# A one added to the normalised input carries the biases, the first table comes back into the score rows, and the transposed second table is added there

## The chip, the cores and the metric

One core of a Trainium2 chip runs the whole program. The metric is the device time of one execution in microseconds (us). A core has five engines with queues of their own: TensorE (PE in the rows; PEld is its loading of weights), VectorE (DVE), ScalarE (ACT), GpSimd (POOL) and SyncE (SP), which issues most transfers between DRAM and the on-chip memory SBUF. TensorE writes into eight banks of another memory, PSUM (PS0 to PS7), which VectorE and ScalarE empty. Engines wait for one another by semaphores.

## The reference, cut to what matters

An image batch of 2 x 32 x 32 tokens with 64 channels goes through an attention-like block over windows of 8 x 8 tokens, and then through a mixture of eight experts. The first block, per window b, with 8 heads h of width 32 and P = 64 positions o, i:

```python
t = x @ W_prep + b_prep            # x normalised over its channels; t holds q_n, q, k, k_m, v
bias, pat_n, pat_m = _spatial(intrinsic)   # tables by the relative position of o and i
score = bias[None]
score = score + jnp.einsum('bhod,ohid->bohi', q_n, pat_n)     # second table
score = score + jnp.einsum('bhod,bhid->bohi', q, k)
score = score + jnp.einsum('bhid,ohid->bohi', k_m, pat_m)     # first table
mean, std = ...                    # over i, for each o and head
score = (score - mean) / std
out = jnp.einsum('bohi,bhid->bohd', score, v)
... out @ W_fin + b_fin, added to x; then the experts
```

The experts: layer norm, a router that keeps the best two of eight, two products with a GELU between them, a weighted sum, added to the input.

## The kernel before, in words

All 32 windows stay on the chip; two windows make a pair, so there are 16 pairs, in four groups of four. The program has these stages.

1. Head. The input XR comes in four parts on SP's queue; WS (weights), REL (tables) and WV on ScalarE's. VectorE computes mean and variance and a reciprocal root by Newton steps; VectorE (three parts) and ScalarE (one) write the normalised input XN. TensorE transposes the weights (L615), multiplies them into the first table (TAM, `table("tm")`, L520), transposes XN into XF (L628), and computes the rows that the biases add (`bias_terms`, L549 to L558). GpSimd spreads these rows (EB), writes them to DRAM, and SP and GpSimd load them back as BI in 16 small transfers (L316).
2. First table's products (L571 with TAM): 16 tiles of four positions, two at a time, each 128 x 512. ScalarE and VectorE copy them from PSUM to TMG, SP writes each tile to DRAM (`moved`, L339). When all are there (`moved_out`), SP reads them back in another order, rows by position, as TMS (L347): this is a transpose through DRAM. Between the tiles TensorE makes the second table (TAN, L520 and L527) and weight products (L540).
3. Second table's products (L571 with TAN), in eight rounds: two tiles, copied to TNT by ScalarE, mixed with key products (`mixed_keys`, L585, into Y), and the turning of the two tiles before (`turned`, L595: four transposes a tile). VectorE adds BI to each turned tile and writes the score rows SCN (L1099). Between them stand the centred input XC (L604) and a shift of the experts' bias (L507).
4. Score loop, one step per pair t, ordered by `pe_steps(t)`: values of a pair (L669, bank 6), scores of two pairs at every second step (L684, banks 0 and 1), weighted sums (L698). GpSimd adds TMS into SCN, pair after pair, 16 adds (L437). VectorE adds the scores and SCN to SR (L1158). ScalarE copies the values to BV (L974), squares SR (SQ, L980), copies the weighted sums to OR (L986). After every four pairs: sums of the squares (`ss`, L708), a copy by ScalarE (SSB, L993), their transposes (`st`, L760), the variances VB by VectorE, a power by GpSimd (RSC, L455), the scaled result ON by VectorE (L1178), its transposes, the last product, the second layer norm and the router. GpSimd's queue holds the power behind the 16 adds.
5. Experts, 16 rounds: hidden products (L719, L720), GELU by ScalarE (L938), second products (L731), gates. Its first round starts in the last step of the loop.

The order of each queue is that of the code. A use of a PSUM bank waits until the use before it is emptied; `make_plan` lists the uses in order and counts these waits.

## Time and profile before

| what | value |
|---|---|
| runs | 201.16, 201.94, 205.39 us; median 201.94 |
| profiled execution | 203.32 us, its span 201.5 us |
| mean granted TensorE clock | 0.975 |
| TensorE busy | 174.9 us (87%) |
| ScalarE busy | 117.9 us (59%) |
| VectorE busy | 108.1 us (54%) |
| GpSimd busy | 85.9 us (43%) |

The span goes from the first to the last instruction of the core; the time of the run holds what lies around it too. The busy share is a mean over stages with different limits: in one stage TensorE works without a gap, in another it waits for a power on GpSimd. The granted clock is that of TensorE: 1.00 is 2.4 GHz, 0.50 is 1.2.

### The profile page before, as it was taken

To read this page: it belongs to the slowest core of one execution; us is meant where nothing else is said; L and a number is where in the kernel's file an instruction comes from. 1 tells how busy PE (TensorE), PEld (TensorE's weight loads), DVE (VectorE), ACT (ScalarE), POOL (GpSimd) and SP (SyncE) were. 2 spreads that over 40 slices of the span, in tenths; PEclk is the share of its full clock that TensorE was granted. 3 is DMA by queue.
4 is the path that set the end of the run, shared out by engine and by line. 5 is a ranking of instruction groups with operands and counts; after the bars stand their busy time and mean duration, and the time that the engine had idled before them with its cause. 6 is when DMAs were issued, how large, how long until landed. Compare 5 with 4: busy or idle time off the path is not lost.

```text
span 201.5 us, 4321 instructions
## 1 busy us (share of the span) xinstructions
PE 174.9 (87%) x1582; PEld 108.6 (54%) x1582; DVE 108.1 (54%) x296; ACT 117.9 (59%) x233; POOL 85.9 (43%) x130
## 2 busy tenths in 40 slices
PE   0519999999998799936995999999999999999983
PEld 0417554654555575626854856575556665655531
DVE  1594258445546525207386955196928773874323
ACT  2244397446453798808596497546666566676730
POOL 6120549040001999993866638481910073031000
PEclk9999999999999999985999789999999999999999
DMA  6930276969991002000300000000000000000000
GB/s 146 245 119 0 90 239 210 335 163 220 220 218 23 0 3 88 20 0 3 102 5 0 2 5 0 0 0 0 3 26 0 0 3 28 0 2 0 29 0 26
DMA packets 10868, 12.96 MB, mean 64 GB/s; under 512 B 2512, under 2 KB 8216, under 8 KB 10848
## 3 DMA queue, kind: packets, MB, share of 16 engines
q1 hardware_dynamic: 9936, 11.73, 22.2%
q10 hardware_dynamic: 528, 0.85, 1.5%
q0 software_dynamic: 384, 0.11, 0.5%
q8 instruction: 13, 0.21, 0.4%
q14 instruction: 7, 0.06, 0.1%
HBM read 7.94 MB, written 4.75 MB: 63 GB/s over the span
## 4 chain that ended last, share of the span: by engine, by line
PE 67%; POOL 14%; DVE 8%; DMA 3%; issue 3%; ACT 3%; SPq 1%; DVEq 0%; ACTq 0%; POOLq 0%
PE PS L731 13%; POOL SCN L437 10%; PE PS L571 9%; PE PS L719 7%; PE PS L720 6%; PE PS L805 4%; PE PS L585 4%; PE PS L780 4%; PE PS L595 3%; DMA XR<-in_x 3%; POOL RSC L455 3%; PE PS L628 2%; PE PS L604 2%; PE PS L769 2%; PE PS L698 1%
## 5 line engine op out<-in xcount | busy, mean ns | idle before, releaser
L938 ACT ACTIVATE HR<-PS,B1P 128x512 f32<-128x512 f32 x64 | 39.0, 693 | 5.0 <-PE PS L720 4.9
L731 PE MATMUL PS<-HR,W2s 128*64 128x512 f32 x128 | 31.0, 605 | 0.0
L437 POOL TENSOR_TENSOR SCN<-SCN,TMS 128x512 f32<-128x512 f32 x16 | 19.7, 1284 | 21.7 <-DVE SCN L1099 21.7
L719 PE MATMUL PS<-X,W1H 128*128 128x512 f32 x64 | 27.5, 430 | 0.0
L720 PE MATMUL PS<-X,W1L 128*128 128x512 f32 x64 | 25.8, 404 | 0.0
L443 POOL COPY PW<-PG 128x512 f32<-128x512 f32 x16 | 10.4, 684 | 34.1 <-DVE PG L1187 33.9
L1019 ACT ACTIVATE GB<-PS 128x512 f32<-128x512 f32 x16 | 9.6, 598 | 23.0 <-PE PS L805 23.0
L455 POOL TENSOR_TENSOR RSC<-VB,NHALF 128x32 f32<-128x32 f32 x4 | 21.9, 5463 | 0.3
L1158 DVE TENSOR_TENSOR SR<-PS,SCN 128x512 f32<-128x512 f32 x16 | 10.7, 685 | 13.6 <-PE PS L684 11.5
L974 ACT ACTIVATE BV<-PS 64x256 f32<-64x256 f32 x32 | 12.2, 380 | 7.6 <-PE PS L669 7.3
L731 PEld LDWEIGHTS PS<-HR,W2s 128*64 128x64 f32 x128 | 7.8, 136 | 13.3 <-issue 12.3
L719 PEld LDWEIGHTS PS<-X,W1H 128*128 128x128 f32 x64 | 12.6, 197 | 3.2 <-issue 0.8
L1139 DVE SCALAR_TENSOR_TENSOR GM<-PS,B,GB 128x512 f32<-128x512 f32 x12 | 9.0, 751 | 9.3 <-ACT GB L1019 7.9
L720 PEld LDWEIGHTS PS<-X,W1L 128*128 128x128 f32 x64 | 12.7, 198 | 2.2
L921 ACT ACTIVATE TNT<-PS 128x512 f32<-128x512 f32 x16 | 8.7, 594 | 8.8 <-PE PS L571 8.8
L805 PEld LDWEIGHTS PS<-IDN,PW 128*128 128x128 f32 x64 | 6.7, 140 | 13.2 <-issue 13.2
L1078 DVE TENSOR_SCALAR Y<-PS,YB 128x512 f32<-128x512 f32 x8 | 6.2, 772 | 12.7 <-PE PS L585 12.7
L669 PE MATMUL PS<-WV,XC 64*64 64x128 f32 x128 | 10.6, 285 | 2.3 <-ACT BV L974 2.2
L980 ACT ACTIVATE SQ<-SR 128x512 f32<-128x512 f32 x16 | 10.1, 630 | 2.4 <-DVE SR L1158 2.1
L698 PE MATMUL PS<-BV,SR 128*64 128x66 f32 x256 | 11.2, 230 | 0.0
L805 PE MATMUL PS<-IDN,PW 128*128 128x128 f32 x64 | 10.5, 286 | 0.8 <-ACT GB L1019 0.8
L986 ACT ACTIVATE OR<-PS 128x264 f32<-128x264 f32 x16 | 6.2, 390 | 7.9 <-DVE ON L1178 5.9
(149 smaller groups left out, 321.8 us busy)
## 6 DMA issues: line engine op xcount, KB each, us to landing
moved<-TMG SPq DMA_DIRECT2D x16, 256.0 KB, 2.9
TMS<-moved SPq DMA_DIRECT2D x16, 256.0 KB, 8.0
W1R<-in_W SPq DMA_DIRECT2D x4, 256.0 KB, 4.0
XR<-in_x SPq DMA_DIRECT2D x4, 128.0 KB, 4.7
W1E<-in_W SPq DMA_DIRECT2D x2, 256.0 KB, 6.2
W2s<-in_W SPq DMA_DIRECT2D x1, 512.0 KB, 3.7
out<-XR SPq DMA_DIRECT2D x4, 128.0 KB, 1.8
REL<-in_rel ACTq DMA_DIRECT2D x2, 225.0 KB, 5.1
```

The lines of the kernel that those rows point to most:

```text
L437: G.tensor_tensor(pair, pair, TMS[:, t, :], ALU.add).then_inc(scn_ready, 1)
L455: G.tensor_tensor(RSC[:, :, :, :].rearrange("p q h g -> p (q h g)"), vb, NHALF[:, :], ALU.pow).then_inc(rsc_ready, 1)
L571: last = nc.tensor.matmul(PS[before[(kind, 2 * m + r)][0]][32 * u:32 * u + 32, :], XF[rows, :, token], window, start=True, stop=True)
L669: m = nc.tensor.matmul(ps[C * g:C * g + C, b * P:b * P + P], XC[rows, lo:lo + WT], WV[rows, g * P:g * P + P], start=True, stop=True)
L698: m = nc.tensor.matmul(dst, SR[t % 3][:, (2 * h + b) * C:(2 * h + b) * C + C], BV[t % 3][:, b, h, :, :].rearrange("p g d -> p (g d)"), sta ...
L719: nc.tensor.matmul(ps[:, :], W1H[:, col:col + P], X2[:, j * 512:j * 512 + 512], start=True, stop=False)
L720: end(nc.tensor.matmul(ps[:, :], W1L[:, col:col + P], X2[:, j * 512:j * 512 + 512], start=False, stop=True), "h", n)
L731: m = nc.tensor.matmul(ps[d * C:d * C + C, :], W2s[:, 2 * (2 * ep + d) + c, :], HR[(4 * u + 2 * c + d) % 8][:, :], start=(c == 0), stop=(c ...
L805: m = nc.tensor.transpose(ps[:, q * P:q * P + P], PW[:, a % 4, q, :, :].rearrange("p d c -> p (d c)"), IDN[:, :])
L938: A(HR[n % 8][:, :], PS[b][:, :], ACT.Gelu, bias=B1P[:, col:col + 1]).then_inc(bank_drained[b], 1)
L974: last = A(BV[tv % 3][g * C:g * C + C, :, :, g, 0:HD].rearrange("p b h d -> p (b h) d"), PS[6][g * C:g * C + C, 0:256].rearrange("p (n d) ...
L1158: V_.tensor_tensor(SR[t % 3][:, :].rearrange("p (h b o) -> p h b o", h=4, b=2), PS[t % 2][:, :].rearrange("p (h b o) -> p h b o", h=4, b=2 ...
```

## The change

The weights are centred (each channel of the input has mean zero over its 64 channels, so subtracting the mean over the channels from the weights changes no product) and get the bias divided by 64 in every row. XF is the normalised transposed input plus one, so that its products with the weights hold the bias. `bias_terms`, YB, EB, the DRAM scratch of the bias and its 17 transfers go. The position bias (RB) is added into the second table by TensorE with SEL. The second table is made before the input is transposed, in banks 4 to 7. The input's last two parts come on ScalarE's queue, the weights and tables on SP's; GpSimd normalises the last part.

The first table's tiles are read back from DRAM into SCN itself, not into TMS. The copies of the second table's products (TNT) take the memory of TMG, so TensorE, ScalarE and VectorE wait for `moved_out` before them. All second products come first, then all key products, all centred inputs, the shift, the first values and scores, and last the 16 turned tiles. Of these VectorE adds twelve into SCN; four are copied by ScalarE (HOP) and added by GpSimd. GpSimd's 16 adds go. Values are computed for two pairs at a time, on the two halves of the array, into banks 6 and 7, with four buffers BV.

```diff
-    for m in range(9):
-        if m < 8:
-            plan += [(("n", 2 * m + r), r, 1) for r in range(2)]
-            plan += [(("yk", 2 * m + r), 4 + r, 1) for r in range(2)]
-        if m >= 1:
-            plan += [(("s", 2 * m - 2 + r), 2 + r, 1) for r in range(2)]
...
+    for m in range(8):
+        plan += [(("n", 2 * m + r), 2 * (m % 2) + r, 1) for r in range(2)]
+    for m in range(8):
+        plan += [(("yk", 2 * m + r), 4 + 2 * (m % 2) + r, 1) for r in range(2)]
+    plan += [(("xc", j), j, 1) for j in range(NG)]
+    plan += [(("b1", r), 4 + r, 1) for r in range(2)]
+    plan += [(("v", 0), 6, 1), (("v", 1), 7, 1), (("score", 0), 0, 1), (("score", 1), 1, 1)]
+    plan += [(("s", tile), 2 + tile % 4, 1) for tile in range(16)]
...
     if t < NPAIR:
-        if t == 0:
-            s.append((("v", 0), 6, 1))
+        if t % 4 == 2 and t >= 6:
+            s.append((("st", (t - 6) // 4), 5, 1))
         if t % 2 == 0:
-            s += [(("score", t), 0, 1), (("score", t + 1), 1, 1)]
-        if t + 1 < NPAIR:
-            s.append((("v", t + 1), 6, 1))
+            s += [(("score", t), 0, 1), (("score", t + 1), 1, 1)] if t else []
+            if t + 2 < NPAIR:
+                s += [(("v", t + 2), 6, 1), (("v", t + 3), 7, 1)]
...
-        return s + late(6, (("st",), 5)) + late(10, (("on", 0), 7), (("on", 1), 5)) + late(15, (("lg",), 6)) \
-            + late(11, (("y",), 7)) + late(14, (("x2",), 6))
+        return s + late(10, (("on", 0), 4), (("on", 1), 7)) + late(14, (("x2",), 5)) \
+            + late(11, (("y",), 4)) + late(15, (("lg",), 5))
...
+            def weights():
+                ps = begin("wt")
+                nc.tensor.matmul(ps[:, :], IDN[:, :], BPS[:, :].unsqueeze(2).to_broadcast([P, SLOT, C]),
+                                 start=True, stop=False)
+                pe.wait_ge(wprep_in, 16)
+                for n_ in range(SLOT):
+                    m = nc.tensor.matmul(ps[:, n_ * C:n_ * C + C], WS[:, n_ * P:n_ * P + P], CEN[0:C, 0:C],
+                                         start=False, stop=(n_ == SLOT - 1))
+                end(m, "wt")
...
-                A(XF[:, 8 * j:8 * j + 8, :].rearrange("p w o -> p (w o)"), PS[b][:, :],
-                  ACT.Copy).then_inc(bank_drained[b], 1)
...
+                A(XF[:, 8 * j:8 * j + 8, :].rearrange("p w o -> p (w o)"), PS[b][:, :], ACT.Copy,
+                  bias=1.0).then_inc(bank_drained[b], 1)
...
-            for t in range(NPAIR):
-                if t % 2 == 0:
-                    pool.wait_ge(moved_in[t // 2], 32)
-                pair = SCN[:, t, :, :, :].rearrange("p b h o -> p (b h o)")
-                G.tensor_tensor(pair, pair, TMS[:, t, :], ALU.add).then_inc(scn_ready, 1)
+            pool.wait_ge(moved_in, N_MOVED)
+            for k in range(4):
+                tile = 4 * k + 2
+                part = SCN[:, :, :, :, 4 * tile:4 * tile + 4].rearrange("p t b h u -> p (t b) h u")
+                pool.wait_ge(*drained("s", tile))
+                G.tensor_tensor(part, HOP[k % 2][:, :].rearrange("p (h u w) -> p w h u", h=4, u=4), part,
+                                ALU.add).then_inc(hop_added, 1)
...
+            dve.wait_ge(moved_in, N_MOVED)
+            for tile in range(16):
+                if tile % 4 == 2:
+                    continue
+                b = before[("s", tile)][0]
+                dve.wait_ge(*filled("s", tile))
+                part = SCN[:, :, :, :, 4 * tile:4 * tile + 4].rearrange("p t b h u -> p (t b) h u")
+                V_.tensor_tensor(part, PS[b][:, :].rearrange("p (h u w) -> p w h u", h=4, u=4), part,
+                                 ALU.add).then_inc(bank_drained[b], 1)
```

How the order of the queues moves, at three places. First TensorE from the first table's products to the start of the loop. Before (the first rounds of eight; L571 are table products, L585 keys, L595 turned tiles, L604 the centred input):

```order
L571 MATMUL PS<-TAM,XF 32x512 x32
L571 MATMUL PS<-TAN,XF 32x512 x8
L585 MATMUL PS<-XF,AT 64x512 x4
L604 MATMUL PS<-CEN,XN 128x128 x4
L571 MATMUL PS<-TAN,XF 32x512 x8
L585 MATMUL PS<-XF,AT 64x512 x4
L595 MATMUL PS<-IDN,TNT_122 128x128 x4
L595 MATMUL PS<-IDN,TNT_123 128x128 x4
```

The same place now (L553 are table products, L568 keys, L585 the centred input, L489 the shift, L599 values, L615 scores, L578 turned tiles):

```order
L553 MATMUL PS<-TAM,XF 32x512 x32
L553 MATMUL PS<-TAN,XF 32x512 x64
L568 MATMUL PS<-XF,AT 64x512 x32
L585 MATMUL PS<-CEN,XN 128x128 x16
L489 MATMUL PS<-LNB,W1E 128x1 x16
L599 MATMUL PS<-WV,XC 64x128 x8
L615 MATMUL PS<-Y,XF 64x4x64 x8
L578 MATMUL PS<-IDN,TMG 128x128 x64
```

The eight rounds of mixed pieces have become one run of each kind, and the first of the second table's products waits for `moved_out`.

Second, TensorE in the loop around the first sums of squares. Before (L708 are the sums, L684 the scores, L669 values, L698 weighted sums, L760 the transposes of the sums SSB):

```order
L708 MATMUL PS<-SQ,ONES_59 32x512 x4
L684 MATMUL PS<-Y,XF 64x4x64 x8
L669 MATMUL PS<-WV,XC 64x128 x4
L698 MATMUL PS<-BV_111,SR_108 64x66 x8
L760 MATMUL PS<-IDN,SSB 128x128 x4
```

Now (L691 sums, L741 their transposes, L615 scores, L599 values, L681 weighted sums):

```order
L691 MATMUL PS<-SQ,ONES_59 32x512 x4
L741 MATMUL PS<-IDN,SSB 128x128 x4
L615 MATMUL PS<-Y,XF 64x4x64 x8
L599 MATMUL PS<-WV,XC 64x128 x8
L681 MATMUL PS<-BV_117,SR_108 64x66 x8
```

The transposes have moved from behind the scores, the values and a weighted sum to ahead of them.

Third, GpSimd before the loop's first power. Before (L437 are the adds into the score rows, L451 the first step of the variance):

```order
L426 MEMSET BV_111 64x8
L437 TENSOR_TENSOR SCN<-SCN,TMS 128x512 x16
L451 TENSOR_SCALAR VB<-VB 128x32
```

Now:

```order
L410 MEMSET BV_119 64x8
L418 TENSOR_TENSOR SCN<-HOP_92,SCN 128x128x4
L418 TENSOR_TENSOR SCN<-HOP_93,SCN 128x128x4
L418 TENSOR_TENSOR SCN<-HOP_92,SCN 128x128x4
L418 TENSOR_TENSOR SCN<-HOP_93,SCN 128x128x4
L433 TENSOR_SCALAR VB<-VB 128x32
```

Sixteen adds over whole pairs have become four, in runs of four elements.

## Rows read from the trace of the kernel before

**Rows 1.** The chain of waits in order of time: start us, duration us, engine and work.
```profile
2.17 6.28 DMA XR<-in_x
...
14.16 3.97 PE PS L628 x16
...
21.33 2.04 PE PS L571 x23
...
113.76 0.73 PE PS L719
```

**Rows 2.** The timeline: start us, duration us, engine, line, operation; idle before and its releaser.
```profile
31.75 1.19 PE L571 MATMUL PS<-TAN,XF 64*32 64x512 f32 x16
...
65.99 0.69 DVE L1158 TENSOR_TENSOR SR<-PS,SCN 128x512 f32<-128x512 f32 x1 [1.54 <-POOL SCN L437]
```

**Rows 3.** The timeline of the head, 0 to 10 us.
```profile
1.78 0.78 POOL L377 DMA_DIRECT2D RB<-in_rel  x1 [0.25 <-issue]
...
2.58 1.11 POOL L379 DMA_DIRECT2D LNB<-in_ln_b  x2
...
5.67 1.08 PE L615 MATMUL PS<-IDN,WS 64*128 64x64 f32 x8 [5.67 <-DMA WS<-in_W_prep]
...
8.02 1.89 PE L520 MATMUL PS<-REL,WT__81 32*128 32x225 f32 x16 [1.27 <-ACT WT__81 L886]
```

**Rows 4.** The timeline of TensorE around the second table, 23 to 27 us.
```profile
23.30 0.66 PE L520 MATMUL PS<-REL,WT__81 32*128 32x225 f32 x8
...
25.04 2.09 PE L571 MATMUL PS<-TAM,XF 64*32 64x512 f32 x32
```

**Rows 5.** The timeline of SP's queue, 20 to 62 us: issues of transfers.
```profile
23.21 6.17 SPq L339 DMA_DIRECT2D moved<-TMG  x8
...
33.31 4.46 SPq L339 DMA_DIRECT2D moved<-TMG  x8
40.26 11.61 SPq L347 DMA_DIRECT2D TMS<-moved  x16
```

**Rows 6.** Windows of 2 us: busy us by engine, PEclk, DMA share, GB/s.
```profile
36.00:38.00 2.00, 2.00 (x24) 1.04 (x16) 0.67 (x1) 1.70 (x3) 0.00 (x0) 1.00 1.03 381
...
90.00:92.00 2.00, 0.00 (x0) 0.00 (x0) 1.14 (x4) 0.69 (x2) 0.82 (x1) 0.50 0.00 0
...
96.00:98.00 2.00, 2.00 (x29) 1.89 (x27) 0.88 (x2) 1.94 (x6) 2.00 (x1) 0.90 0.00 0
```

**Rows 7.** The chain of waits in one of the eight rounds.
```profile
44.20 1.17 PE PS L571 x12
45.37 1.02 PE PS L585 x8
```

**Rows 8.** The costliest groups: shapes, count, busy us, mean ns, idle before.
```profile
L437 POOL TENSOR_TENSOR SCN<-SCN,TMS 128x512 f32<-128x512 f32 x16 | 19.7, 1284 | 21.7 <-DVE SCN L1099 21.7
...
L974 ACT ACTIVATE BV<-PS 64x256 f32<-64x256 f32 x32 | 12.2, 380 | 7.6 <-PE PS L669 7.3
...
L980 ACT ACTIVATE SQ<-SR 128x512 f32<-128x512 f32 x16 | 10.1, 630 | 2.4 <-DVE SR L1158 2.1
...
L986 ACT ACTIVATE OR<-PS 128x264 f32<-128x264 f32 x16 | 6.2, 390 | 7.9 <-DVE ON L1178 5.9
```

**Rows 9.** The timeline of the score loop, 76 to 93 us.
```profile
76.38 1.09 PE L684 MATMUL PS<-Y,XF 64*64 64x256 f32 x16
...
76.83 0.59 ACT L993 ACTIVATE SSB<-PS 128x512 f32<-128x512 f32 x1
...
77.30 0.61 PE L669 MATMUL PS<-WV,XC 64*64 64x128 f32 x8
...
85.35 5.47 POOL L455 TENSOR_TENSOR RSC<-VB,NHALF 128x32 f32<-128x32 f32 x1
...
90.86 1.43 DVE L1178 TENSOR_TENSOR ON<-OR,RSC 128x256 f32<-128x256 f32 x4 [7.72 <-POOL RSC L455]
...
92.25 1.11 PE L760 MATMUL PS<-IDN,SSB 128*128 128x128 f32 x4 [4.82 <-ACT SSB L993]
```

More of the change, by code:

```diff
@@ L511, in shift_bias, with warm @@
                                 end(m, "b1", r)
+            def weights():
[7 more added lines that the diff above has]
+                end(m, "wt")
+            def warm():
+                for _ in range(8):
+                    nc.tensor.matmul(PS[7][:, 0:P], IDN[:, :], IDN[:, :], start=True, stop=True)
             def table(kind):
@@ L671, in values @@
-                end(m, "v", t)
+                        for a in range(2):
+                            rows = slice(C * a, C * a + C)
+                            lo = (2 * (t + a) + b) * WT
+                            m = nc.tensor.matmul(PS[6 + a][C * g:C * g + C, b * P:b * P + P], XC[rows, lo:lo + WT],
+                                                 WV[rows, g * P:g * P + P], start=True, stop=True)
+                            if b + g == 2:
+                                end(m, "v", t + a)
@@ new lines, in _ @@
+            dve.wait_ge(moved_in, N_MOVED)
+            for tile in range(16):
+                if tile % 4 == 2:
[5 more added lines that the diff above has]
+                                 ALU.add).then_inc(bank_drained[b], 1)
```

446 lines of the change are left out of this document (201 added, 245 removed).

## The prediction

> **What bounds the kernel now.** I read the chain of waits first, since it says which engine the end hangs on in each stretch, and then the timeline at its joints. Four marks cut the run [rows 1, 2]. A, 21.33 us: the first product with the first table. B, 31.75: the first with the second table. C, 65.99: the first score sum SR. D, 113.76: the first hidden product of the expert stage, which the change leaves as it is; from D to the end of the span (201.5) are 87.7 us.
>
> Up to A the chain is the input: its last quarter lands at 8.45, the transposes of the normalised input run from 14.16 to 18.13, and the bias rows fill TensorE until 21.33 [rows 1]. From A to C the chain stays on TensorE, piece behind piece [rows 7]. From C to D no engine is full. ScalarE has the most to do: for two pairs it makes four value copies, two squares and two row copies [rows 8], 4 x 0.38 + 2 x 0.63 + 2 x 0.39 = 3.56 us. But the largest gap comes from GpSimd: its 16 adds of 1.28 us hold back the power of 5.47 us, which starts at 85.35, and VectorE waits 7.72 us for it before ON at 90.86 [rows 8, 9]. The eleventh sum follows ON, at 92.29, so C to there is 26.3 us, and from there to D 21.5.
>
> **The change, mark by mark.** I work out how much each mark moves.
>
> A. The bias rows go (21.33 - 18.13 = 3.2 us), the second table comes in ahead of the transposes, and the weights now need matmuls, with constants that GpSimd makes behind six DMA issues instead of three. Those issues: 1.78 + 0.78 + 5 x 0.56 [rows 3] = 5.4; the constants, five small instructions whose prices no row gives, 1.5 by estimate (0.3 each, half an issue): 6.9. The weights: 8 transposes took 1.08 [rows 3]; matmuls of full precision show as two instructions each, so 2 x 1.08, and 0.9 for the bias operand in front: 10.0. Two copies, at 0.59 as the one in [rows 9]: 11.2. The first table 1.89: 13.1. The second table took from 23.30 to 25.04, 1.7 us, at full clock [rows 4]; the first table's 16 instructions took 1.89 in the head, where the same eight at 23.30 took 0.66, so the head runs slow, and I take 2.7, between 1.7 and the 3.5 of half clock: 15.8. The transposes, paced by their inputs in 3.97 now, I put at 2.0: 17.8, and a copy of 0.6: **A at 18.4, -2.9**. The input no longer decides: two quarters go on ScalarE's queue, and even from a landing at 8.45 the transposes could start at 14.2. Bounds: with weights at 2.2 and tables at 1.3 and 1.7, all at full clock, 15.9; with the second table at 3.5 and transposes at 3.97, 21.2. So -5.4 to -0.1; the steps lie in one chain, so the middle is likeliest.
>
> B. TensorE now stops at a barrier before the second table's products: all 16 tiles of the first must be in DRAM, because the turned tiles take over their memory. Before, B was A + 10.4, and the write-out ended 8.5 us later beside it. The products themselves: 8 x 1.05 (two groups of eight matmuls in 2.09 [rows 4]), 0.7 for the weight products, half a microsecond for banks: done at A + 9.7. The write-out: first issue at A + 1.9; the last eight tiles took from 33.31 to 40.26 with the wait for landing [rows 5], 2.10 MB at the 381 GB/s seen in 36 to 38 [rows 6] is 5.5 us, which leaves 1.45 for start and landing. All sixteen: 1.9 + 1.45 + 11.0, plus 0.5 because four table copies on ScalarE hold the fifth tile back: A + 14.9. SP no longer stops for the bias loads, so nothing else is in the queue. TensorE idles 5 us where it had none. **B at A + 14.9 against A + 10.4: +4.5**. Bounds: with no hold-back A + 14.3; at the mean pace of the last eight tiles, 2 x 6.95 + 1.9 = A + 15.8.
> The page "DMA: Bandwidth & Descriptors" of the Trainium skill (section "Where 436 GB/s comes from") puts the ceiling of the ports at 435 GB/s; by it the write-out would take an estimated 9.6 us and B come 1.4 us earlier, and the total would be 200.4. The window shown has 381.
>
> C. The pieces between B and C are the same, in another order, 34.2 us now. Kept together, the second table's products should cost 1.05 a group as the first's do, not the 1.17 of its rounds [rows 7]: -0.9. The keys' products (1.02 behind another kind [rows 7]) I put 0.05 lower each, between no gain and the 0.12 of the tables: -0.4. Values for two pairs on the two halves of the array: 4 matmuls took 0.61 [rows 9], eight alternating I put at 0.95: -0.3 here.
> "TensorEngine Tiling (Array Packing)" of the Trainium skill (section "Key Properties") says that a change of the tiling mode drains the engine. By that rule keys save the full 0.12 and the total is 201.2; the trace has the tables' difference, and no row with keys in succession.
> Against that stands the clock. TensorE stood still for 4.8 us before 92.25 [rows 9], about as long as the new barrier holds it; the granted clock was 0.50 (1.2 of 2.4 GHz) in 90 to 92 and 0.90 in 96 to 98 [rows 6], back at full some 4 us after work resumed. Four microseconds at half clock lose 2.0: +2.0 (bounds 0 and 2.5). The reading back of the table, 11.6 us of issues now [rows 5], goes straight into the score rows and has from B until the turning, 23 us, so it stays hidden. The adds move onto VectorE, one for one, with twelve of its sixteen left; four go through ScalarE and GpSimd. Their tail: a copy of 0.6 and a GpSimd add of 1.28 behind the last tile [rows 8], against one GpSimd add now: +0.5; if runs of four elements double GpSimd's price, four adds take 10.3 us where the turning takes about 8.2, +2.8. **C: +0.9 on B's side** (bounds -1.6 to +3.7).
>
> D. GpSimd's 16 adds leave the loop, so the power starts when its input is there. But the transpose of the square sums now stands in front of the next score products on TensorE, and waits for ScalarE's copy (0.59, the last thing in its queue [rows 9]). ScalarE then runs dry until transposes 0.5, scores 1.09 and values 0.95 are through: 2.5 us, where before the scores at 76.38 went ahead of that copy. So from C: three pairs 3 x 3.56, copy 0.6, dry 2.5 = 13.8; the power 5.5, and 1.3 by estimate for the two short steps before it and the hand-overs: 20.6; ON 1.43: 22.0; then the second such stop, copy, transposes and scores 0.6 + 0.5 + 1.1: the eleventh sum at 24.2, against 26.3: -2.1. TensorE stops some 3 us there too, so the half-clock stretch behind it, worth 2 us of the 21.5, likely half remains: -0.5 after ON's wait and one stop at the third copy. **D: -2.6** (bounds -8 and +5, the rivals). Paired values shorten only TensorE, which waits there.
>
> Sum: -2.9 + 4.5 + 0.9 - 2.6 = -0.1 us. The profiled execution took 203.32 (span 201.5 and 1.8 around it), so 203.2 on its terms; the median of the runs shown is 201.94, 1.4 lower, so **201.8 us**. Changes below 2% (4.0 us) count as no change, about what a measurement of this kernel can tell.
>
> **Rivals.** *Faster, the loop runs free.* If ScalarE's queue is never dry, five pairs, a copy and ON take 5 x 3.56 + 0.6 + 1.4 = 19.8 us to the eleventh sum instead of 26.3, and the 2.0 of half clock behind it go: -8.5 where I have -2.6. With A 1.2 earlier, since the head is priced at a slow clock: 201.8 - 5.9 - 1.2 = 194.7. For it: every wait behind the power, 7.72 and what follows, hangs on GpSimd. Against it: the transposes' new place. Chance 0.24.
> *Slower, three stops in the loop each drop the clock.* The transposes of the square sums come three times before D; each makes TensorE wait for ScalarE 2 to 3 us. The stop at 87.4 took the clock to 0.50; if stops half as long do so as well, each costs 2 us behind it, six in all where I count one: +5, 206.8. It decides at whether the granted clock falls in the loop before the eleventh sum. For it: the clock's fall [rows 6]. Against it: no row shows a stop of 2 to 3 us doing it. Chance 0.26.
> *The adds don't leave the path*: GpSimd's four, at twice the price, bound the turning: +2.3, 204.1, inside the forecast's side. It and the forecast (no change) have 0.50 together.
>
> So faster 0.24, same 0.50, slower 0.26. The range takes the bounds of A and the tail from the forecast and reaches towards both rivals: 195.2 to 208.2.
>
> **What would show it.** First table product near 18 us (later than 20: the weights' chain is mis-sized). A TensorE gap of about 5 us before the second table, ending with the last landing of the moved tiles, and clock 0.50 behind it; without the gap B's term is wrong. VectorE's first SR at 67 to 70. In the loop, transposes of the square sums waiting for ScalarE, and ON waiting for the power less than 7.7 us. First hidden product at 112 to 115. If it comes before 108 the loop term failed, if after 118 the clock.

## The result and the profile after

The changed kernel took 213.73 us (median of four runs, 211.62 to 215.86) against 203.62, 1.050 times the kernel before (interval 1.041 to 1.059). In a second sitting it took 210.43 us (208.15 to 215.86) against 205.63 (201.85 to 208.31): 1.023 (1.015 to 1.031). So it is slower, by some 5 to 10 us, where no change was forecast. Single executions of one kernel differ here by up to 4% (the kernel before took 200.7 to 209.4 us over all sittings); a time given is the median of all runs, and a ratio with an interval leaves out the slower executions of either kernel, so it need not be the quotient of the medians beside it. The argument below therefore rests on distances inside the profiles, over several of them, and sets against each other only times of one sitting.

The four marks of the prediction, a fifth (E, the first second product of the experts) and the end of the span, in us, for the two kernels' first profiles (201.5 and 210.0):

| mark | before | after | moved by, since the mark ahead | forecast |
|---|---|---|---|---|
| A, first product with the first table | 21.26 | 20.87 | -0.4 | -2.9 |
| B, first product with the second | 31.75 | 37.55 | +6.2 | +4.5 |
| C, first score sum | 65.99 | 72.94 | +1.2 | +0.9 |
| D, first hidden product | 113.69 | 119.68 | -1.0 | -2.6 |
| E, first second product of the experts | 120.22 | 128.72 | +2.5 | 0 |
| end of the span | 201.5 | 210.0 | 0.0 | 0 |

The sum is +8.5. From E on the two are alike: 81.3 us each. Four terms share the miss: A and E came out 2.5 worse each, B 1.7, D 1.6 (in this one profile of D; over all of them it came out better, below).

The chain of waits after, from the head to the second table (start, duration, engine and work), answers to [rows 1]:

```profile
11.57 2.63 PE PS L518 x24
...
16.45 3.44 PE PS L642 x16
...
20.87 2.12 PE PS L553 x29
...
23.76 1.89 ACT TAN L862 x4
...
33.40 3.81 DMA moved<-TMG
37.20 0.35 issue
37.55 9.74 PE PS L553 x89
```

The bias rows (3.2 us) are gone, but from 6.9 to 19.9 the chain is now TensorE's weights, tables and transposes (the last two L518 and L642), with one copy between them. At B the last tile's landing holds it; the list of waits names that as the one wait of 6.9 us:

```profile
PE PS L553 <- DMA moved<-TMG: 6.9, 1, 6.9
```

The windows after (busy us by engine, the granted clock, DMA share, GB/s), to be read against [rows 6]:

```profile
16.00:18.00 2.00, 2.00 (x16) 1.62 (x9) 0.47 (x1) 0.00 (x0) 1.69 (x6) 0.50 0.00 0
...
24.00:26.00 2.00, 1.84 (x38) 0.93 (x30) 1.38 (x2) 2.00 (x6) 0.00 (x0) 1.00 1.04 387
26.00:28.00 2.00, 2.00 (x44) 1.06 (x38) 0.35 (x2) 1.93 (x7) 0.00 (x0) 1.00 0.69 254
...
34.00:36.00 2.00, 0.00 (x0) 0.00 (x0) 0.00 (x0) 0.00 (x0) 0.00 (x0) 0.50 0.85 314
...
40.00:42.00 2.00, 2.00 (x32) 0.57 (x16) 1.06 (x2) 0.89 (x2) 0.00 (x0) 0.50 1.08 221
```

TensorE is at half clock (0.50, 1.2 GHz) in the head and again behind the barrier. The write-out reaches 387 GB/s in one window and 254 and 314 in others; the forecast had 381 throughout. The Trainium skill's ceiling of 435 GB/s ("DMA: Bandwidth & Descriptors", section "Where 436 GB/s comes from") was not reached: the estimate made by it was the further off.

The timeline after at three places (start, duration, engine, operation, idle before and its releaser), which answers to [rows 2, 9] and shows what stands between D and E:

```profile
72.94 1.29 DVE L1146 TENSOR_TENSOR SR<-PS,SCN 128x512 f32<-128x512 f32 x2 [1.28 <-POOL SCN L418]
...
94.01 1.43 DVE L1166 TENSOR_TENSOR ON<-OR,RSC 128x256 f32<-128x256 f32 x4 [3.14 <-POOL RSC L437]
...
124.17 1.07 PE L691 MATMUL PS<-SQ,ONES 128*32 128x512 f32 x8 [2.40 <-DVE XR L1182]
```

ON waits 3.14 us for the power instead of 7.72: that part did what was forecast. The third row is a wait that the kernel before has not got: the last sums of squares stand 2.40 us behind VectorE's step L1182, which empties the product y. In the kernel before they start without a wait:

```profile
117.18 1.07 PE L708 MATMUL PS<-SQ,ONES 128*32 128x512 f32 x8
```

### The profile page after: what moved, and what is told of

It reads as the page before. It is cut to its first block, busy times and chain, and to the rows that moved or that the text cites. A ratio compares the mean times of both kernels' runs of the same rounds, so it can differ in the third digit from the quotient of the medians.

```text
span 210.0 us, 4283 instructions
## 1 busy us (share of the span) xinstructions
PE 179.1 (85%) x1590; PEld 113.5 (54%) x1590; DVE 107.9 (51%) x298; ACT 114.5 (55%) x225; POOL 70.5 (34%) x104
## 4 chain that ended last, share of the span: by engine, by line
PE 65%; ACT 10%; DVE 6%; POOL 6%; issue 6%; SPq 2%; DMA 2%; DVEq 0%; ACTq 0%; POOLq 0%
PE PS L714 12%; PE PS L553 7%; PE PS L702 6%; PE PS L703 6%; PE PS L615 4%; PE PS L786 4%; PE PS L568 4%; PE PS L578 3%; POOL RSC L437 3%; PE PS L761 3%; SPq L331 2%; ACT BV L912 2%; DMA moved<-TMG 2%; PE PS L585 2%; PE PS L642 2%
## 5 line engine op out<-in xcount | busy, mean ns | idle before, releaser
L437 POOL TENSOR_TENSOR RSC<-VB,NHALF 128x32 f32<-128x32 f32 x4 | 21.8, 5461 | 0.3
L418 POOL TENSOR_TENSOR SCN<-HOP,SCN 128x512 f32<-128x512 f32 x4 | 6.2, 1553 | 44.5 <-ACT HOP L923 44.5
L1146 DVE TENSOR_TENSOR SR<-PS,SCN 128x512 f32<-128x512 f32 x16 | 10.6, 687 | 17.8 <-PE PS L615 14.5
L862 ACT ACTIVATE TMG<-PS 128x512 f32<-128x512 f32 x16 | 10.1, 648 | 16.0 <-PE PS L553 16.0
L553 PE MATMUL PS<-TAN,XF 64*32 64x512 f32 x128 | 10.9, 816 | 6.9 <-DMA moved<-TMG 6.9
L681 PE MATMUL PS<-BV,SR 128*64 128x66 f32 x256 | 11.7, 242 | 2.6 <-issue 2.2
L681 PEld LDWEIGHTS PS<-BV,SR 128*64 128x64 f32 x256 | 9.8, 150 | 5.5 <-issue 5.4
L840 DVE COPY TMG<-PS 128x512 f32<-128x512 f32 x8 | 5.6, 698 | 12.2 <-PE PS L553 12.2
L615 PE MATMUL PS<-Y,XF 64*64 64x256 f32 x128 | 11.2, 478 | 0.4 <-DVE SR L1146 0.4
```

The costliest lines, as they stand in the source:

```text
L437: G.tensor_tensor(RSC[:, :, :, :].rearrange("p q h g -> p (q h g)"), vb, NHALF[:, :], ALU.pow).then_inc(rsc_ready, 1)
L553: last = nc.tensor.matmul(PS[before[(kind, 2 * m + r)][0]][32 * u:32 * u + 32, :], XF[rows, :, token], window, start=True, stop=True)
L615: m = nc.tensor.matmul(dst, XF[rows, 2 * (t + a) + b, :], Y[rows, 4 * g:4 * g + 4, t // 2, C * b:C * b + C], start=True, stop=True)
L681: m = nc.tensor.matmul(dst, SR[t % 3][:, (2 * h + b) * C:(2 * h + b) * C + C], BV[t % 4][:, b, h, :, :].rearrange("p g d -> p (g d)"), sta ...
L1146: V_.tensor_tensor(SR[t % 3][:, :].rearrange("p (h b o) -> p h b o", h=4, b=2), PS[t % 2][:, :].rearrange("p (h b o) -> p h b o", h=4, b=2 ...
```

## The experiments

Two theories were set against each other. *Parts*: the time is the sum of separate places (head, barrier, reading back, shared bank), each of which can be undone alone. *Clock*: stops anywhere lower TensorE's clock, and the loss is what runs at 1.2 GHz behind them.

**The kernels again, unedited.** A second profile of each:

> The changed kernel again, unedited, to see what differs between two profiles of it. Theory: the distances between the marks repeat (first table's products to second table's 16 to 17 us, second table's to first score sum 34.5 to 35.5, first hidden product to first second product 9.0), while the first mark moves between 19.4 and 23.3 us, as it did in the four kernels that share its head, by where in the head the clock rises; total 208 to 214 us. Rival: the distances themselves scatter by over 2 us, and the differences of single profiles say nothing on the change.

> The kernel before again, unedited, for a second profile. Theory: the distances between its marks repeat as the three kernels that share them have it (first to second table's products 10.5 us, from there to the first score sum 34.2 to 34.4, 47.6 to 50.3 to the first hidden product, 6.3 to 7.0 to the first second product) and its first product with the first table lies between 20.4 and 22.7 us, no later than the changed kernel's 19.4 to 23.3. Rival: it starts at under 20 us here, and the change's head is later than before's.

Measured: after 210.43 us, before 208.14 (one run). With the profiles of the later kernels that share a stretch, the distances are:

| stretch | kernels with before's code | kernels with the change's code |
|---|---|---|
| start to A | 20.43 to 22.68 (5) | 19.41 to 23.27 (7) |
| A to B | 10.46 to 10.52 (4) | 15.24 to 18.19 (6) |
| B to C | 34.24 to 34.33 (4) | 34.31 to 35.39 (6) |
| C to D | 47.64 to 51.83 (4) | 42.36 to 46.74 (8) |
| D to E | 6.29 to 7.00 (4) | 8.87 to 9.26 (7) |

(In parentheses the number of profiles.) In three stretches the two ranges lie apart: A to B and D to E are longer now, C to D shorter. The head's ranges cover each other: the change's is no shorter. C to D scatters by 4 us on either side, and the scatter goes with the clock. The mean granted clock of that stretch and its length in us, one number for each profile:

| mean granted clock, C to D | 1.00 | 0.96 | 0.92 to 0.93 | 0.89 | 0.84 to 0.85 |
|---|---|---|---|---|---|
| before's code | | | 47.64, 47.70 | 50.24 | 51.83 |
| the change's code | 42.36 | 43.94 | 44.47, 45.06 | 45.28, 45.39 | 46.69, 46.74 |

The first and the second profile of the changed kernel stand at its two ends:

```profile
72.94:119.68 46.74, 37.36 (x557) 27.35 (x557) 21.42 (x56) 30.83 (x72) 20.77 (x16) 0.85 0.09 24
```

```profile
73.51:115.87 42.36, 31.90 (x557) 24.00 (x557) 21.12 (x55) 30.73 (x72) 20.07 (x16) 1.00 0.09 27
```

At a like clock the change's loop is shorter by 2.6 to 5.1 us. The same stop of 2.2 us at the start of the loop was followed by half clock in the first profile of the changed kernel and not in its second; each one's window behind it:

```profile
74.00:76.00 2.00, 2.00 (x31) 1.33 (x30) 0.23 (x1) 1.28 (x3) 0.00 (x0) 0.54 0.00 0
```

```profile
74.00:76.00 2.00, 1.69 (x37) 1.48 (x41) 0.80 (x2) 1.62 (x3) 0.00 (x0) 1.00 0.00 0
```

The second profile of before kept 0.50 from 92 to past 104, where [rows 6] had 0.90 by 96 to 98, and came to D 4.5 us later. So the first expectation fell in part: B's and D's distances scatter by more than 2 us, and only what the ranges of the table part can be argued from one profile.

**Head 1: without the warm-up.**

```diff
-            pe.wait_ge(consts_ready, 1)
-            warm()
```

> The changed kernel without its eight warm-up products of the head (they are part of the change: TensorE works from 1.6 to 5.4 us on nothing that is used). Theory: the warm-up is what makes the clock fall in the head. With it the granted clock is 0.50 from about 9.3 to 19.2 us; before, TensorE began at 5.67 us, then stood still for 4.25 us, and the clock stayed at 1.00 throughout. So without it the clock stays at 1.00 up to 20 us, the table products and the transposes get shorter, the first product with the first table starts at 17.5 to 18.5 us instead of 20.87, and the total falls by 2.5 to 3.5 us. Rival: the gaps between the head's pieces make the clock fall whatever went ahead of them; then the first product with the first table stays at 20.5 to 21 us and the total within 0.5 us of the changed kernel's.

Measured: A at 21.18; 210.55 us against 205.74, 1.034 (1.026 to 1.043). A came near the rival's 20.5 to 21, but as the sum of two opposite effects: the weights' 16 products took 3.67 us without the warm-up and 2.41 with it, and the transposes 1.97 against 3.44 in the chain above. So the theory is refuted, the warm-up does not lower the clock, and it serves the weights. The run also showed how the head's clock must be read: in this profile the column has 1.00 up to 34 us, the slow weights included. The transposes (TensorE's timeline; the first row is the changed kernel with the shared bank mended, whose clock column also has 1.00 here, the second the one with the filler below, where by the column full clock came back at 15.8) say it most plainly:

```profile
18.60 3.68 PE L642 MATMUL PS<-IDN,XN 128*128 128x128 f32 x16
```

```profile
16.28 1.97 PE L642 MATMUL PS<-IDN,XN 128*128 128x128 f32 x16
```

The same 16 instructions take 3.68 or 1.97 us: half or full clock. Over the seven profiles with the changed head A follows the moment at which they speed up: 19.41 where that is 15.8, 20.87 where it is 19.6, and 22.05 to 23.27 in the five where all 16 transposes are slow. The kernel before depends on it too: eight products of its bias rows took 1.69 us in the profile with the earliest A (20.43, the kernel of barrier 1 below) and 3.17 in the one with the latest (22.68, the kernel before with y in bank 4):

```profile
17.57 1.69 PE L554 MATMUL PS<-REL,BB 128*8 128x225 f32 x8
```

```profile
18.11 3.17 PE L554 MATMUL PS<-REL,BB 128*8 128x225 f32 x8
```

**Head 2: the second table made where it was.**

```diff
-            table("tn")
...
                 pattern("m", m)
+                if m == 1:
...
+                    table("tn")
```

> The changed kernel with the second table made where it was before, behind the first four tiles of the first table's products, instead of ahead of the input's transposes. Theory: its 24 products cost 2.6 us in the head at half clock, and they lie on the way to the first product; that comes at 17.5 to 19 us where the head's clock is low until 19 (20.87 before this edit), the write-out starts as much earlier, and the total falls by 1.5 to 2.5 us. Rival: the input's normalisation (its last part ends at 13.4 us) and the low clock decide: the first product comes within 0.7 us of where it was and the total is the same within 0.7.

Measured: A at 19.66, A to B 16.42, 207.89 us (207.78 to 209.22) against 210.43 for the changed kernel in the same sitting, 1.015 (1.009 to 1.022) of the kernel before. The theory's direction held, with A 1.2 earlier than in the first profile of the changed kernel, though A's scatter is wider than that; the transposes still took 3.65 us, at half clock. In the three later profiles with this edit A is at 19.14, 19.61 and 21.00, so the four lie some 2 us under the mean of the changed head (19.9 against 21.9).

**Barrier 1: alone, in the kernel before.**

```diff
+            pe.wait_ge(moved_out, 16 * 16)
             for m in range(9):
                 if m < 8:
                     pattern("n", m)
```

> The kernel before with one part of the change alone: TensorE waits for all moved tiles to be in DRAM before its first product with the second table. Theory: that product moves from 10.4 us to 18.5 to 19.5 us behind the first with the first table (the write-out ends at 40.26 there), the clock falls to 0.50 in the gap and 3 to 6 us beyond, and as the reading back is not delayed and nothing else covers the gap, the first score sum comes 10 to 11 us later, the total 9 to 11 us. Rival: the clock holds; then 8 us at the first score sum and in the total. Second rival: the loop, held by GpSimd's adds and the power, absorbs part of it: the total grows by 4 to 6 us only.

Measured: 216.12 us against 205.63, 1.045 (1.035 to 1.055), so some +9 us; B at A + 19.33, and C at 76.10, 10.1 later than in [rows 2]. TensorE's timeline at B:

```profile
39.76 2.03 PE L571 MATMUL PS<-TAN,XF 64*32 64x512 f32 x16 [8.58 <-DMA moved<-TMG]
```

2.03 us where the same 16 instructions took 1.19 in [rows 2]. The theory held in both parts: 8.8 us of standing and 2.1 more from B to C at half clock.

**Barrier 2: standing without the half clock.** The results of the 22 products are not used.

```diff
+            for _ in range(22):
+                nc.tensor.matmul(PS[4][:, 0:P], IDN[:, :], IDN[:, :], start=True, stop=True)
             pe.wait_ge(moved_out, 16 * 16)
```

> The changed kernel with 22 products of 128 x 128 into an unused bank (their results are not used), which TensorE makes in front of its wait for the moved tiles; at 0.27 us each they fill 6.0 of the 6.5 us in which it stands still. Theory: the barrier's price has two parts, the standing still (which stays) and the half clock behind it (which goes): the first product with the second table stays at 37.5 us, the clock stays at 1.00 from 32 to 44 us, the eight rounds take 8.5 to 9 us instead of 10.95 and the total falls by 2 to 2.5 us. Rival: the rounds are paced by the copies of ScalarE and VectorE, not by the clock: they still take 10.5 to 11 us and the total falls by less than 0.5 us.

Measured: B at A + 16.41, unmoved; from there to the first key product 8.72 us, where the changed kernel's first profile has 10.88 and the six others with the barrier 9.81 to 10.78, and the clock at 1.00; 208.82 us against 205.74, 1.027 (1.019 to 1.036), with one run of the ten at 424.49 us, which is not explained. The changed kernel itself was not run in this sitting, so the gain in the total is not shown. The windows:

```profile
34.00:36.00 2.00, 0.48 (x11) 0.29 (x17) 0.00 (x0) 0.00 (x0) 0.00 (x0) 1.00 0.12 43
...
40.00:42.00 2.00, 2.00 (x40) 0.78 (x32) 1.21 (x3) 1.12 (x2) 0.00 (x0) 1.00 1.07 233
```

So half clock is 1.1 to 2.2 us of the barrier's price, 2.2 in the first profile (2.0 forecast). At full clock the eight groups cost 1.09 us each: keeping them together saved 0.08 a group against the 1.17 of [rows 7], not 0.12. The rule that a change of the tiling mode drains the engine (the Trainium skill, "TensorEngine Tiling (Array Packing)", section "Key Properties") would have given the keys the full 0.12; they show 0.99 a group in succession against 1.02.

**Barrier 3: split by tile.**

```diff
-            pe.wait_ge(moved_out, 16 * 16)
...
             for tile in range(0, 16, 2):
+                act.wait_ge(moved_out[tile // 2], 32)
                 store_turn(act, act_copy, tile)
```

> The changed kernel with the one semaphore for all 16 moved tiles split into eight, one for two tiles; each copy of a product with the second table waits only for the two tiles whose memory it takes, and TensorE waits for none. Theory: the barrier costs its 6.5 us of standing still and 2 to 2.5 us of half clock behind it. Then the first product with the second table starts at 31 us instead of 37.55, the clock stays at 1.00 from 30 to 45 us, and the next limit is the reading back, which still ends at about 57 us: the turned tiles can be added from there, the first score sum comes at 66 to 67 us instead of 72.94, and the total falls by 6 to 7 us. Rival: the write-out paces the products instead (each pair of products waits for its tiles to land, the write-out gets slower beside them), the first score sum comes at 69 to 71 us and the total falls by 2 to 4 us. Second rival: the loop gives the gain back by stops that lower the clock; then the first score sum is at 66 to 67 us but the total falls by less than 4 us.

Measured: 207.82 us (204.14 to 212.74) against 205.74, 1.010 (0.999 to 1.021). B at A + 9.83, and no half clock there. But C came 49.3 us behind A, only 2.8 less than the 52.1 of the changed kernel's first profile, 1.8 less than in its second:

```profile
61.37 3.25 DVE L1093 TENSOR_TENSOR SCN<-PS,SCN 128x512 f32<-128x512 f32 x5 [6.56 <-DMA SCN<-moved]
```

The next limit is the reading back, as the theory said, but at 61.4 us where it had 57. The 57 was read too early: in the changed kernel's first profile the transfers still show in the windows 56 to 58 (153 GB/s) and 58 to 60 (10 GB/s). Here they show two microseconds later, 1.3 of which is the later A. The reading back lands 39.2 us behind A, no sooner than with the barrier, since it cannot begin before the write-out ends; VectorE adds no turned tile before all of it has landed; and the half clock comes back behind TensorE's stop there (0.69, 0.50 and 0.96 in 62 to 68). The rival's slower write-out did not come: it took 14.5 us from first issue to last landing, as with the barrier. The prediction held the reading back to be hidden. It was, only because the barrier had made everything behind it late.

**The shared bank: mended in the changed kernel, put into the kernel before.**

```diff
-            + late(11, (("y",), 4)) + late(15, (("lg",), 5))
+            + late(11, (("y",), 4 if t < 15 else 7)) + late(15, (("lg",), 5))
```

> The changed kernel with the second block product y of step 15 in bank 7 instead of bank 4. Theory: with values in banks 6 and 7 the change put y into the bank of the sums of squares, so that the last sums wait for VectorE to empty y, and VectorE comes to that only behind the router's steps: TensorE stands still 2.40 us in front of them, and the clock falls behind that stop. In the other bank the stop goes, the way from the first hidden product to the first second product is 6.5 us as before instead of 9.0, and the total falls by 2.5 us. Rival: what comes next (the gates, which need the same VectorE steps) waits as long, and the total falls by 0 to 0.7 us.

```diff
-            + late(11, (("y",), 7)) + late(14, (("x2",), 6))
+            + late(11, (("y",), 7 if t < 15 else 4)) + late(14, (("x2",), 6))
```

> The kernel before with one part of the change alone: the product y of step 15 in bank 4, that of the sums of squares, instead of bank 7. Theory: the wait for VectorE's emptying of y behind the router's steps appears here too; the way from the first hidden product to the first second product grows from 6.5 us to 9 to 10.5, and the total by 2.5 to 4 us. Rival: in the kernel before VectorE is early enough there, the way stays within 0.7 us of 6.5 and so does the total.

Measured in the changed kernel: D to E 5.06 us instead of 8.87 to 9.26, -4.0: 2.4 of standing and the half clock behind it; 205.98 us (204.13 to 208.21) against 205.74 (200.70 to 208.47), 0.987 (0.974 to 1.000); but the lowest runs give 1.017, so the time settles nothing here and the distance is the evidence. TensorE's timeline with the bank mended, at the place of the wait:

```profile
122.12 1.06 PE L691 MATMUL PS<-SQ,ONES 128*32 128x512 f32 x8
```

In the kernel before the same wait appears, shorter:

```profile
122.80 1.06 PE L708 MATMUL PS<-SQ,ONES 128*32 128x512 f32 x8 [1.63 <-DVE XR L1194]
```

D to E is 8.07 there, 1.5 over 6.53; the total shows nothing (208.88 us against 205.63, 1.000, 0.989 to 1.011). Theory right on the mechanism, too high on the size: there the hidden products run at half clock, so they last until nearer VectorE's step.

**The adds' tail.** Tiles 0, 4, 8 and 12 through ScalarE and GpSimd.

```diff
-                tile = 4 * k + 2
+                tile = 4 * k
```

> The changed kernel with tiles 0, 4, 8 and 12 going through ScalarE and GpSimd instead of 2, 6, 10 and 14. Theory: the first score sum waits 1.28 us for GpSimd's add of tile 14; with tile 12 as the last of GpSimd's that wait goes, and VectorE's own adds set the end: the first score sum comes 23.2 to 23.4 us behind the first key product instead of 24.5 (24.49 to 24.51 in four profiles). Rival: VectorE's adds, now with the last three tiles in a row, end later by as much; 24.3 us or more.

Measured: 23.90 us from the first key product to C, between the two expectations: the wait for GpSimd went, but VectorE's own adds now end only 0.2 us ahead of the score sum, so 0.6 of the 1.28 is gained. The one run, 211.31 us, tells nothing of so little.

**The loop: the transposes of the sums behind the scores.**

```diff
-        if t % 4 == 2 and t >= 6:
-            s.append((("st", (t - 6) // 4), 5, 1))
...
-        return s + late(10, (("on", 0), 4), (("on", 1), 7)) + late(14, (("x2",), 5)) \
+        return s + late(6, (("st",), 5)) + late(10, (("on", 0), 4), (("on", 1), 7)) + late(14, (("x2",), 5)) \
```

> The changed kernel with the transposes of the square sums behind the next scores, values and weighted sum again, where they stood before. Theory (the prediction's): ahead of the scores they make TensorE wait about 2 us for ScalarE's copy, ScalarE and VectorE run dry behind that, and VectorE's variance, which is queued behind the next score sum, gets later too. Put behind, the stop of 2.0 us in front of them goes, ON comes 18 to 18.7 us behind the first score sum (19.7 to 21.3 in the four profiles so far of this loop with the transposes ahead), and the first hidden product 41 to 43 us behind it (42.4 to 46.7 so far); the total falls by 1.5 to 3 us. Rival: the power sets the loop's pace either way; ON stays at 19.7 us or later and the total the same within 1 us.

Measured: ON at C + 17.8 (19.7 to 22.4 in the eight profiles with the transposes ahead), D at C + 40.6 (42.4 to 46.7). The power starts at C + 12.3 instead of C + 15.6 (14.2 to 16.9 in the eight). The stop, in the changed kernel and what stands there now:

```profile
84.72 0.66 PE L741 MATMUL PS<-IDN,SSB 128*128 128x128 f32 x4 [2.03 <-ACT SSB L979]
```

```profile
86.40 0.66 PE L739 MATMUL PS<-IDN,SSB 128*128 128x128 f32 x4
```

The theory held, with more than it had: VectorE's variance stands behind a score sum in its queue, and that waits for scores which the transposes held back. The total was 208.80 us against 205.48, 1.034 (1.027 to 1.042): in this profile A came at 23.26 and B at A + 18.2, and ate the gain. The changed kernel was not run in this sitting, so the expected fall of the total is not shown.

**The loop's gain alone, in the kernel before.** VectorE makes GpSimd's last four adds.

```diff
-            for t in range(NPAIR):
+            for t in range(12):
...
+                if 1 <= t <= 4:
+                    own = 11 + t
...
+                    pair = SCN[:, own, :, :, :].rearrange("p b h o -> p (b h o)")
+                    step(V_.tensor_tensor(pair, pair, TMS[:, own, :], ALU.add))
```

> The kernel before with the last four of GpSimd's sixteen adds into the score rows made by VectorE, in steps 1 to 4 of the loop where it waits for scores; nothing else is changed. Theory: what the change gains in its loop is that the power starts when its input is there. Here it starts 4.5 to 5 us earlier too (4 x 1.23 us of adds), at 14.5 to 15 us behind the first score sum instead of 19.4, ON at 20 instead of 24.9 to 25.1, TensorE's stop of 4.8 us ahead of it gets shorter than 2.5 us, and the total falls by 3 to 6 us: the change's gain without its losses. Rival: GpSimd's power is not the limit but ScalarE's queue is; the power starts earlier, the first hidden product stays 47 us or more behind the first score sum, and the total the same within 1 us.

Measured: 201.20 us against 205.48, 0.991 (0.985 to 0.997). ON waits less and comes at C + 21.7:

```profile
88.16 1.43 DVE L1187 TENSOR_TENSOR ON<-OR,RSC 128x256 f32<-128x256 f32 x4 [4.93 <-POOL RSC L455]
```

D is at C + 44.6, 3.1 less than in [rows 1, 2], at the lower end of the theory's 3 to 6 in the profile; in the times the gain is under it, some 2 us (0.7 to 3.1 by the interval). TensorE's stop ahead of ON's transposes is 2.0 us instead of 4.8. The power started 3.1 us earlier, not 4.5 to 5, since GpSimd's twelve adds took 16.62 us instead of 14.8.

**Together.** The edits of barrier 3, head 2, the bank, the tail and the loop.

> The changed kernel with five edits together: the semaphore of the moved tiles split in eight, the second table's making behind the first four tiles, y of step 15 in bank 7, GpSimd's tiles 0, 4, 8, 12, and the transposes of the square sums behind the scores. Theory: the pieces add up, with the reading back as the limit of the first score sum: first product with the first table at 18 to 21 us, first score sum 48 to 49 us behind it (52 without the edits, 44.7 before the change), 42 us to the first hidden product, 6.5 us to the first second product: a total of 199 to 203 us, the same as the kernel before within 2%. Rival: what is saved ahead is lost to stops that lower the clock in the loop; a total of 205 us or more.

Measured: 199.37 us against 205.48, 0.983 (0.977 to 0.988): faster than the kernel before by 1 to 2%, and below every run of the changed kernel, which was run in other sittings. A 19.14, B at A + 12.3, C at A + 51.3 (2.5 more than expected: the reading back lands later, and half clock stands behind it), D at C + 41.2, E at D + 5.1. Against the changed kernel's means three stretches carry it: the loop with 3.8 us (41.2 against 45.0), the bank with 4.0, and the head, where A is 2.8 earlier. A to C is no shorter than there.

**Together, with the half clock at the reading back filled.** The results of the 14 products are not used.

```diff
+                if tile == 4:
+                    pe.wait_ge(*drained("v", 0))
+                    for _ in range(14):
+                        nc.tensor.matmul(PS[6][:, 0:P], IDN[:, :], IDN[:, :], start=True, stop=True)
                 turned(tile)
```

> The kernel of the five edits with 14 products of 128 x 128 into bank 6 (results not used) between the fourth and the fifth turned tile, where TensorE stands still 3.8 us until the reading back has landed. Theory: the clock stays at 1.00 there instead of falling to 0.50 from 61 to 66.5 us, but the turning is paced by VectorE's adds of 0.62 to 0.86 us each; the first score sum moves by 0 to 1.5 us, the total by 0 to 2 us below that of the kernel of the five edits. Rival: the half clock sets the pace of the turning; the first score sum comes 2 us or more earlier, and so does the total.

> The kernel of the five edits again, unedited, beside the one with the filler. Expected as in its first sitting: 198 to 202 us, 0.975 to 0.99 of the kernel before.

Measured: 197.40 us (195.46 to 200.24) with the filler, 199.38 (197.82 to 200.72) without, before 205.78 (201.45 to 208.84). By the medians that is 0.959 and 0.969, by the lowest runs 0.970 and 0.982; nine of the kernel before's eleven runs lie above 205 us, so the second pair is the fairer. The filler's gain is 2.0 us by the medians, 2.4 by the lowest runs. From VectorE's first add into the score rows to the first score sum are 7.5 us with the filler, 9.6 and 8.7 in the two profiles without. The windows there, without (that profile) and with:

```profile
64.00:66.00 2.00, 2.00 (x12) 2.00 (x11) 1.05 (x2) 0.56 (x1) 0.00 (x0) 0.50 0.00 0
```

```profile
64.00:66.00 2.00, 2.00 (x18) 1.77 (x17) 2.00 (x4) 0.16 (x1) 1.81 (x2) 1.00 0.00 0
```

In the same 2 us TensorE makes 18 instructions instead of 12 and VectorE four adds instead of two: the turning is paced by TensorE at half clock, by VectorE at full. C is 49.1 us behind A with the filler, 51.3 and 48.0 in the two profiles without, so neither the profiles nor the times, near the 2 us where the two meet, tell theory and rival apart. D to E, with the bank mended, is 6.15 and 6.07 us here against the 5.1 above: the bank's gain is 3 to 4 us.

## Why the prediction was wrong

- **A, -2.9 against -0.4.** The order of the steps was right (constants done at 6.7 where I had 6.9, weights at 10.3 for 10.0, both tables at 16.5 for 15.8). The sized step that failed is the transposes: 2.0 was taken, 3.44 measured, because TensorE was still at half clock; that is 1.4 of the 2.5 us, and the tables and the hand-over behind the last copy are most of the rest. The prediction's own sign, A later than 20, laid such a miss to the weights; they were on time. I read a clock of 1.00 in the head of the kernel before and took "the head runs slow" for the tables alone. Its 16 table instructions of 1.89 [rows 3] beside 0.66 for eight [rows 4] already said that the column is not to be trusted there. In the kernel before, TensorE stood still 4.25 us for the input ahead of the transposes, so a slow clock in the weights and the table cost nothing there; in the changed one the head is TensorE's own chain, and what was moved into it ahead of the clock's rise pays for it. The 3.2 us for the bias rows came from an execution whose clock rose early: over the five profiles of that head they take 3.1 to 5.2 us. Over all profiles A is the same in both kernels (21.5 and 21.9 in the mean).
- **B, +4.5 against +6.2.** The mechanism was right, the gap and the half clock behind it stood where they were put, and the barrier alone slowed the kernel before. Mis-sized: the write-out, 14.45 us from first issue to last landing instead of 13.0, at 254 to 387 GB/s instead of 381. The dip to 254 follows ScalarE's four table copies in the chain (23.76 to 25.65), whose hold-back was put at 0.5; why the last tiles went at 311 to 314 is not shown. (The products' sum, 8 x 1.05 + 0.7 + 0.5, is 9.6 and not 9.7; B does not hang on it.)
- **C, +0.9 against +1.2.** That the sum came out so close is in part luck, since its errors cancel. Half clock cost 2.2 in this profile (2.0 forecast, 1.1 to 2.2 over all). The tables' groups saved 0.08 each (0.12, of which eight are 1.0 and not the 0.9 in the sum) and the keys' 0.03 (0.05). The tail, put at +0.5, cost nothing: the first score sum waits 1.28 us for GpSimd where it waited 1.54 in [rows 2]. GpSimd's four adds took 1.49 to 1.58 us each, not twice 1.28, so the rival in which they bound the turning did not come about; moving them earlier gained 0.6 us. "Stays hidden", for the reading back, held only behind the barrier.
- **D, -2.6 against -1.0 in the first profile, and about -4 over all** (means of the ranges' profiles, 49.4 before and 45.0 after). The step is right: the power starts sooner, which the kernel before with four adds moved shows alone, and the transposes ahead of the scores take part of it away, which moving them back shows. At a like clock the loop gains 2.6 to 5.1 us. "Three stops each drop the clock" happened in some executions and not in others: in the first profile the loop ran at a mean clock of 0.85, in the second at 1.00 behind stops of the same length, and it took 4.4 us more. So the slower rival's mechanism is real, but it is not what sets the changed kernel apart: the kernel before has it too (0.84 to 0.93).
- **E, 0 against +2.5.** "The expert stage, which the change leaves as it is" is the step that failed outright: a wait put at nothing. The edit gave banks 6 and 7 to the values, so y went from bank 7 to bank 4, and the diff shows that in one digit. I priced the wait of every engine and never asked which use had stood in each bank before. It costs 3 to 4 us in the changed kernel with the clock behind it.

Neither of the two theories wins alone: in the first profile the barrier's 8.4 us are 6.2 by which B is later and 2.2 of clock, the bank's 4.0 are 2.4 and 1.6. So the step that decided is no single one: the barrier was seen and priced too low, the bank was not seen, the head was priced at a clock that it had not got, and together they outweigh the loop's gain. D at 119.7 is past the 118 behind which the prediction would have blamed the clock in the loop; it was late because B was. What stays open is the size of the whole: the two sittings give 2.3% and 5.0%, with intervals that do not meet. The distances' means add up to some 5 us. The changed kernel's two profiles, one of each sitting, differ by 3.6 us (spans of 210.0 and 206.4): 4.4 is the loop at the lower clock and 1.0 lies between B and C, against a head that was 1.6 the faster. What makes the clock fall in one execution and not in another was not shown.

## What to carry to other kernels

When banks or buffers are dealt out anew, list for each use what stood there before and who empties it: the wait appears far from the edit. Reusing memory under a transfer makes its landing a barrier: count one semaphore for each piece, and price the half clock behind the gap as well. A stretch that was covered by a wait is cheap only while the wait is there; before moving work into it, compare durations of the same instruction there and in a stretch at full clock.

## What the runs showed of the hardware

- The clock column can say 1.00 where TensorE runs at half: 16 transposes took 3.68 us at a shown 1.00, 3.68 at a shown 0.50 (the changed kernel's second profile) and 1.97 where the column had risen to 1.00 just before them. Ahead of the column's first change, go by the durations.
- The clock differs from execution to execution of one kernel, in the head (it rose at 15.8 us in one, after 25 in another) and behind equal stops (0.54 or 1.00 behind 2.2 us).
- The clock's price, in one kernel without an edit: the loop took 42.4 us at a mean granted clock of 1.00 and 46.7 at 0.85.
- VectorE's adds from two SBUF operands and GpSimd's delay each other: with four of them in between, GpSimd's twelve adds took up to 1.73 us each (1.27 to 1.29 alone), VectorE's 0.75 to 1.67, where its add of one operand from PSUM takes 0.69:

```profile
L437 POOL TENSOR_TENSOR SCN<-SCN,TMS x12: 1259/1274/1730, 65.1 to 80.5; 128x512 f32<-128x512 f32 x12
...
L1170 DVE TENSOR_TENSOR SCN<-SCN,TMS x4: 750/1093/1672, 68.3 to 74.0; 128x512 f32<-128x512 f32 x4
```

  The Trainium skill's page "SBUF — State Buffer" (section "SBUF: two separate sides") has the two engines share a pair of ports as an exclusive lock, which VectorE's instructions with two SBUF inputs take too; the trace agrees.
